# The setup of a fused attention and expert kernel in another order: stages moved on all five engines, other buffers for the raw W1

## Chip, core and metric

The kernel runs on one core of one Trainium2 chip. A core has a matrix engine (TensorE, PE in the profile), a vector engine (DVE), a scalar engine (ACT), GpSimd (POOL) and a synchronisation engine (SP) whose main work here is to issue transfers. Each engine carries out its own instructions in order and waits for others at semaphores. The metric is the time of one execution in microseconds, as the median of several executions.

## What is computed

For each of 32 sequences ("rows") of 512 tokens with 256 channels the reference does a modulated layer norm, a scan over time followed by a 256x256 matrix, a local convolution with 5 taps, a gated residual, a second modulated layer norm, a router that takes one expert of eight by the row's last token, and the expert's two matrices with a GELU between them:

```python
mod = (_silu(L0_c) @ L0_wmod).reshape(L0_c.shape[0], 6, 1, -1)
h = _layernorm(x, axis=-1) * (1 + ca) + sa
x = x + ga * _L0_attn_ref(h, ...)      # scan @ W.T + b + conv(h)
h = _layernorm(x, axis=-1) * (1 + cb) + sb
x = x + gb * _L0_ffn_ref(h, ...)
# in _L0_ffn_ref, per row:
sel = jnp.argmax(action_probs, axis=-1)
h = gelu(einsum('bsh,bhf->bsf', hidden_states, W1[sel]) + b1[sel])
reasoned = einsum('bsf,bfh->bsh', h, W2[sel]) + b2[sel]
return hidden_states + 0.3 * (reasoned @ Wo + bo)
```

## The kernel before

**The loop.** After a setup, `slot(i)` runs for i = 0 to 32 on every engine. In slot i the rows overlap: row i goes through the expert (`up`, `down`), row i+1 through the second norm and the router, row i+2 through the convolution and its residual, row i+3 through the first norm and the scan. The setup must have brought rows 0 to 2 that far. The first matmul of slot 0 after `mix(2)` is `up(0, 0)` (L1011); it needs the expert's first matrix in `up_w`.

**The expert's matrices.** Matrix products are made at higher precision from split operands: a high part (fp32r) and a low part, the difference. The setup makes these tables for all eight experts e:

- W1: SP loads the raw matrix (`load_w1`, L293, 512 KB) into a buffer `w1_nat(e)`, chosen by the table `W1_AT`; ACT writes the high part (`w1_hi`, L538), POOL the low part (`w1_lo`, L414), both into `split_room[e]` (borrowed from `hid_hi`, `hid_lo`, `g_lo`, `down_w` 0 and 1, `up_w` 0 and 1, and `g_lo` again for e = 7); then SP writes the pair (1 MB) to `up_table` in DRAM (`split_out`, L297). A raw buffer is loaded again only when `w1_lo` has read it.
- W2 times Wo: SP or ACT loads W2 (`load_w2`) into row buffer 3, 4 or 5 of `xr`; PE transposes it (`w2_transposes`, L925); ACT copies it (`w2T_copy`, L544); PE multiplies it by Wo (`comb`, L976, two halves per expert); ACT and DVE make high and low parts in `down_tab`, which stays in SBUF (`down_high`, L552; `down_low`, L787).

When all eight splits have landed in `up_table` and the router has chosen row 0's expert (`sel_ready`, L820), SP reads the choice and fetches the expert into `up_w` (L366) and `down_w` (L369).

**The rows in the setup.** A row's first half is: statistics (`stats1`, L745, DVE), inverse deviation (`norm1`, POOL), normalised x (`xn1_of`, L530, ACT), transposes (`to_channels`, L1051, PE), `h_of` (L638, ACT), scan (L826, DVE), split of S (`s_high` on ACT, `s_low0` on POOL L429, `s_low1` on DVE), `mix` (L991 to L995, PE), convolution (`conv`, L797, DVE, ten steps), `gate1` (L589, ACT), `back_to_tokens` (L1043, PE), residual with its statistics (`residual1`, L809, DVE). The second norm is `norm2` (POOL), `xn2_of` (L530, ACT), `to_channels` (PE), `hid_of` (L615, ACT, writes `hid`), `hid_high` and `hid_low`; then `router_nav`, `nav_of`, `router_logits`, `router`.

**What sets the order.** Each engine has a function `prologue()` in which the stages stand in an order written by hand; SP's stands open in its block. Nothing is rearranged by a compiler. Before the change `hid_of(0)` waits until seven `w1_lo` are done, because expert 6's raw W1 lies in `hid`; `split_out(7)` waits for the eighth.

## Time and profile before

| | us |
|---|---|
| three runs, median | 691.85 (689.66 to 692.11) |
| the profiled execution | 695.64 |
| its span, first to last instruction | 693.6 |
| of it, until the first `up(0, 0)` matmul starts | 93.9 |
| mean granted TensorE clock, share of full | 0.984 |

The profiled execution took 2.0 us more than its span, and 3.8 us more than the median. Times in the rows count from the span's start. "Busy" is the time in which an engine had an instruction in work; a wait is idle time before an instruction, with the event that ended it. DMA share is the mean busy share of the 16 DMA engines.

### The profile page before, as it was taken

The numbers are of one execution on the slowest core, as the hardware profiler recorded it, in microseconds if no ns is written. First come the engines' busy times: TensorE is split into PE (matmuls) and PEld (weight loads), VectorE is DVE, ScalarE is ACT, GpSimd is POOL, SyncE is SP. The second block draws the span as 40 slices with busy tenths as digits, with TensorE's granted clock in tenths as the row PEclk, the third lists the DMA queues.
The fourth block names the chain that finished last, engine by engine and source line by source line (L and its number), as shares of the span: only waits on it lengthen the run. The fifth ranks groups of instructions, "written<-read, shape, count | busy, mean of one in ns | idle before, by whom it ended". The sixth has DMA issues, their size and how long they took to land.

```text
span 693.6 us, 11162 instructions
## 1 busy us (share of the span) xinstructions
PE 663.7 (96%) x3469; PEld 532.2 (77%) x3469; DVE 566.3 (82%) x863; ACT 568.4 (82%) x976; POOL 462.8 (67%) x536
## 2 busy tenths in 40 slices
PE   7996759999999999999999999999999999999996
PEld 7985547777777878778777777787877778777764
DVE  1776729999999999999999999999999999998711
ACT  3677548888888998888888888898898888887753
POOL 2743527777777777777777777777777777776543
PEclk9998979999999999999999999999999999999998
DMA  8989345555555554455555555545455555444451
GB/s 265 311 242 314 125 151 157 179 166 168 183 182 160 144 164 167 162 179 179 159 179 161 175 183 181 155 147 177 147 170 183 171 163 183 154 151 152 152 166 47
DMA packets 55454, 120.58 MB, mean 174 GB/s; under 512 B 5643, under 2 KB 43364, under 8 KB 46180
## 3 DMA queue, kind: packets, MB, share of 16 engines
q1 hardware_dynamic: 51844, 115.65, 52.7%
q10 hardware_dynamic: 3552, 4.23, 2.4%
q8 instruction: 28, 0.46, 0.3%
q14 instruction: 30, 0.25, 0.1%
HBM read 61.12 MB, written 25.19 MB: 124 GB/s over the span
## 4 chain that ended last, share of the span: by engine, by line
PE 90%; ACT 2%; DMA 2%; DVE 2%; POOL 2%; issue 1%; POOLq 0%; SPq 0%; DVEq 0%; ACTq 0%
PE Q L1031 9%; PE Q L1026 9%; PE U L1011 9%; PE U L1013 9%; PE U L1012 8%; PE TR L1051 8%; PE Q L1027 8%; PE Y L995 5%; PE Q L1043 4%; PE Y L991 4%; PE Y L992 4%; PE TR L1043 4%; PE Q L976 2%; PE U L1062 2%; PE Y L948 1%
## 5 line engine op out<-in xcount | busy, mean ns | idle before, releaser
L421 POOL TENSOR_TENSOR g_lo<-g,g_hi 128x512 fp32r<-128x512 f32 x128 | 190.8, 1499 | 148.1 <-ACT g_hi L578 142.5
L797 DVE SCALAR_TENSOR_TENSOR Y<-h,taps,Y 128x512 f32<-128x512 f32 x320 | 222.6, 750 | 2.4
L1011 PE MATMUL U<-hid_hi,up_w 128*128 128x512 f32 x256 | 107.1, 418 | 10.2 <-DMA up_w<-up_table 10.2
L571 ACT ACTIVATE g<-U,up_w 128x512 f32<-128x512 f32 x128 | 88.5, 691 | 28.9 <-PE U L1013 26.1
L1026 PE MATMUL Q<-g_hi,down_w 128*128 128x512 f32 x256 | 109.7, 429 | 0.2
L530 ACT ACTIVATE S<-xr,nmr,rstd 128x256 f32<-128x256 f32 x128 | 66.6, 592 | 42.7 <-POOL S_lo L429 36.3
L1013 PE MATMUL U<-hid_lo,up_w 128*128 128x512 f32 x256 | 101.6, 397 | 0.0
L1012 PE MATMUL U<-hid_hi,up_w 128*128 128x512 f32 x256 | 101.3, 396 | 0.0
L1027 PE MATMUL Q<-g_hi,down_w 128*128 128x512 f32 x256 | 101.1, 395 | 0.0
L826 DVE TENSOR_TENSOR_SCAN S<-keep,h 128x512 f32<-128x512 f32 x64 | 75.2, 1215 | 26.7 <-ACT h L638 26.6
L745 DVE BATCH_NORM_STATS2 st<-xr 128x6 f32<-128x512 f32 x128 | 87.6, 706 | 4.3
L1031 PE MATMUL Q<-g_lo,down_w 128*128 128x512 f32 x256 | 83.7, 408 | 0.7 <-POOL g_lo L421 0.7
L578 ACT CAST g_hi<-g 128x512 fp32r<-128x512 f32 x128 | 80.5, 629 | 3.1
L530 ACT ACTIVATE xn<-xr,nmr,rstd 128x256 f32<-128x256 f32 x128 | 66.5, 591 | 8.2 <-POOL nmr L409 6.0
L407 POOL TENSOR_TENSOR rstd<-rstd,minus_half 128x4 f32<-128x4 f32 x64 | 66.4, 1037 | 0.0
L1011 PEld LDWEIGHTS U<-hid_hi,up_w 128*128 128x128 f32 x256 | 48.8, 191 | 19.2 <-DMA up_w<-up_table 10.7
L1031 PEld LDWEIGHTS Q<-g_lo,down_w 128*128 128x128 f32 x256 | 45.0, 187 | 23.7 <-POOL g_lo L421 14.3
L884 DVE SCALAR_TENSOR_TENSOR rT<-Q,mods,w_raw 128x512 f32<-128x512 f32 x64 | 44.6, 739 | 18.1 <-PE Q L1031 18.1
L429 POOL TENSOR_TENSOR S_lo<-S,S_hi 128x512 fp32r<-128x512 f32 x32 | 54.4, 1699 | 5.0 <-ACT S_hi L565 5.0
L1013 PEld LDWEIGHTS U<-hid_lo,up_w 128*128 128x128 f32 x256 | 48.5, 190 | 11.4
L1012 PEld LDWEIGHTS U<-hid_hi,up_w 128*128 128x128 f32 x256 | 49.0, 191 | 8.8
L1026 PEld LDWEIGHTS Q<-g_hi,down_w 128*128 128x128 f32 x256 | 48.1, 188 | 9.8 <-ACT g_hi L578 0.9
(114 smaller groups left out, 1302.7 us busy)
## 6 DMA issues: line engine op xcount, KB each, us to landing
up_w<-up_table SPq DMA_DIRECT2D x32, 1027.0 KB, 6.6
down_w<-down_tab SPq DMA_DIRECT2D x32, 1024.0 KB, 8.6
xr<-in_L_attn_x_dram SPq DMA_DIRECT2D x32, 512.0 KB, 3.6
out_dram<-xr SPq DMA_DIRECT2D x64, 256.0 KB, 2.2
xr<-in_L_ffn_W_dram ACTq DMA_DIRECT2D x5, 512.0 KB, 9.3
xr<-in_L_ffn_W_dram SPq DMA_DIRECT2D x4, 512.0 KB, 6.9
up_table<-g_lo SPq DMA_DIRECT2D x2, 1024.0 KB, 7.9
up_table<-down_w SPq DMA_DIRECT2D x2, 1024.0 KB, 9.6
```

What stands on the lines that cost most here:

```text
L421: nc.gpsimd.tensor_tensor(g_lo[:, f], g[:, f % 2], g_hi[:, f].bitcast(f32), ALU.subtract).then_inc(g_lo_ready, 1)
L530: nc.scalar.activation(to[:, j], xr[:, r % NX, j], ACT.Identity, bias=nmr[:, j:j + 1], scale=rstd[:, j:j + 1]).then_inc(ready, 1)
L571: nc.scalar.activation(g[:, f % 2], U[f % 2][:, :], ACT.Gelu, bias=up_w[:, i % 2, U_B1 + f:U_B1 + f + 1].bitcast(f32)).then_inc(gelu_out, 1)
L578: nc.scalar.copy(g_hi[:, f], g[:, f % 2]).then_inc(g_hi_ready, 1)
L745: return nc.vector.bn_stats(st[:, k * TPB:(k + 1) * TPB].rearrange("p t s -> p (t s)"), pair)
L797: ins = nc.vector.scalar_tensor_tensor(out=Y[c][:, :], in0=h[:, c, k:k + T], scalar=taps[:, c, k:k + 1], in1=Y[c][:, :], op0=ALU.mult, op1 ...
L1011: mm(U[f % 2][:, :], up_w[:, par, UP + w:UP + w + P], hid_hi[:, par, c], start=(c == 0), stop=False)
L1012: mm(U[f % 2][:, :], up_w[:, par, w:w + P], hid_hi[:, par, c], start=False, stop=False)
L1013: ins = mm(U[f % 2][:, :], up_w[:, par, w:w + P], hid_lo[:, par, c], start=False, stop=(c == DC - 1))
L1026: mm(Q[c][:, :], down_w[:, par, 1, w:w + P], g_hi[:, f], start=(f == 0), stop=False)
L1027: mm(Q[c][:, :], down_w[:, par, 0, w:w + P], g_hi[:, f], start=False, stop=False)
L1031: ins = mm(Q[c][:, :], down_w[:, par, 0, w:w + P], g_lo[:, f], start=False, stop=(f == FC - 1))
```

## The change

**Buffers.** `W1_AT` goes from (0, 1, 2, 3, 1, 2, 1, 2) to (0, 1, 2, 0, 3, 1, 2, 4). Place 0 is `rT`, 1 `hid`, 2 `w1_raw[1]`; place 3 was row 2's x buffer and is now `xn`, and the new place 4 is row 3's x buffer. So `rT` is used twice, `hid` holds experts 1 and 5, expert 6 lies in `w1_raw[1]` and expert 7 in row 3's buffer. Row 2's buffer is free for x once the modulations have been computed, row 3's only when the eighth `w1_lo` is done.

**Order.** Stages in the five `prologue()` functions stand in another order; `gbeta`, `hid_gated`, the output and the second residual become functions of their own, called where they were. The work is the same: each load, split, transpose and product once. In short: W2 of expert 0 and the small vectors are loaded first; the vector transpose comes ahead of the modulations; row 0's first transposes come after two experts' W2 transposes; x of row 2 is loaded before `split_out(0)` and its statistics stand ahead of row 0's residual; `w1_lo(7)` on POOL stands ahead of `hid_low(0)` and `w1_hi(7)` on ACT ahead of `xn2_of(0)`; `stats1(3)` stands ahead of `router(0)` on DVE.

```diff
-        W1_AT = (0, 1, 2, 3, 1, 2, 1, 2)
+        W1_AT = (0, 1, 2, 0, 3, 1, 2, 4)
...
 SyncE
-            sp.wait_ge(s_w1_lo, 4)
-            load_x(2)
...
-            load_w1(6)
-            split_out(3)
...
+                sp.wait_ge(s_mod_mm, 1)
+                load_x(2)
+                split_out(0)
+                split_out(1)
+                split_out(2)
+                load_w1(6)
+                split_out(3)
+
+                sp.wait_ge(s_w2T_mm, 4)
+                load_w1(7)
+                split_out(4)
+                load_router()
+                split_out(5)
+                beta_out()
+                split_out(6)
+
+                sp.wait_ge(s_w1_lo, E)
+                load_x(3)
+                split_out(7)
...
 ScalarE, waits of gate1, xn2_of, hid_of (row 0) and of the gated hid
-                    act.wait_ge(s_w1_lo, 1)
+                    act.wait_ge(s_w1_lo, 4)
-                    act.wait_ge(s_wT, 1)
+                    act.wait_ge(s_w1_lo, 5)
-                    act.wait_ge(s_w1_lo, 7)
+                    act.wait_ge(s_w1_lo, 6)
-                        act.wait_ge(s_w1_lo, E)
+                    act.wait_ge(s_w1_lo, 7)
...
 VectorE
-                residual1(0, 1)
-                down_low(3, 1)
-                conv(1, 0, 3)
...
-                conv(1, 3, 6)
-                stats1(2)
...
                 conv(0, 9, 10)
+                stats1(2)
+                down_low(2, 1)
                 scan(1, 0)
...
+                stats1(3)
+                router(0)
...
 TensorE, end of the prologue
                 pe.wait_ge(hid_ready, DC)
                 to_channels(2, xn1, xn1_ready, t1_done)
+                comb(5, 1)
+                w2_transposes(7)
+                back_to_tokens(1)
+                router_nav(0)
                 comb(6, 0)
-                w2_transposes(7)
                 comb(6, 1)
-                router_nav(0)
+                router_logits(0)
                 comb(7, 0)
-                router_logits(0)
-                back_to_tokens(1)
                 comb(7, 1)
```

SyncE's queue, second half of the setup, before. `xr<-in_L_attn_x_dram` is an x load (row 2, then row 3), `hid`, `w_raw` and `xr` from `in_L_ffn_W_dram` raw matrices, `up_table<-` a split going out.

```order
L285 DMA xr<-in_L_attn_x_dram 128x4x256 [waits s_w1_lo]
L338 DMA wp<-in_L_ffn_Wp_dram 128x2x128
L339 DMA wp<-in_L_ffn_Wp_dram 128x8
L340 DMA bp_sb<-in_L_ffn_bp_dram 1x8
L293 DMA hid<-in_L_ffn_W_dram 128x2x512 [waits s_w1_lo]
L297 DMA up_table<-down_w 128x2048 [waits s_w1_lo]
L344 DMA up_table<-beta 128x8x2 [waits s_beta3]
L293 DMA w_raw<-in_L_ffn_W_dram 128x2x512 [waits s_w1_lo]
L297 DMA up_table<-down_w 128x2048 [waits s_w1_lo]
L285 DMA xr<-in_L_attn_x_dram 128x4x256 [waits s_w2T_mm]
L297 DMA up_table<-up_w 128x2048 [waits s_w1_lo] x2
L297 DMA up_table<-g_lo 128x2048 [waits s_w1_lo]
```

The same queue after the change, from the last raw W1 loads to the last split. Row 2's x is no longer in this stretch, it has moved ahead of the first split; the raw W1 of expert 7 goes to a buffer of its own; x of row 3 stands behind seven splits.

```order
L287 DMA xr<-in_L_attn_x_dram 128x4x256 [waits s_mod_mm]
L299 DMA up_table<-hid_hi 128x2048 [waits s_w1_lo]
L299 DMA up_table<-hid_lo 128x2048 [waits s_w1_lo]
L299 DMA up_table<-g_lo 128x2048 [waits s_w1_lo]
L295 DMA w_raw<-in_L_ffn_W_dram 128x2x512 [waits s_w1_lo]
L299 DMA up_table<-down_w 128x2048 [waits s_w1_lo]
L295 DMA xr<-in_L_ffn_W_dram 128x2x512 [waits s_w2T_mm]
L299 DMA up_table<-down_w 128x2048 [waits s_w1_lo]
L328 DMA wp<-in_L_ffn_Wp_dram 128x2x128
L329 DMA wp<-in_L_ffn_Wp_dram 128x8
L330 DMA bp_sb<-in_L_ffn_bp_dram 1x8
L299 DMA up_table<-up_w 128x2048 [waits s_w1_lo]
```

ScalarE around `hid_of(0)`, before. `S<-xr` is `xn1_of(2)`, the casts are `w1_hi(6)` and `w1_hi(7)`, `hid<-TR` is `hid_of(0)`, `g<-U` `w2T_copy(6)`, `h<-TR` `h_of(2)`, `rT<-Y` `gate1(1)`.

```order
L530 ACTIVATE S<-xr,nmr,rstd 128x256 [waits norm1_ready,S_lo_ready1,S_lo_ready0]
L530 ACTIVATE S<-xr,nmr,rstd 128x256 x3
L538 CAST up_w<-hid 128x1024 [waits s_w1_1]
L552 ACTIVATE down_tab<-Q 128x512 [waits s_comb]
L615 ACTIVATE hid<-TR,mods 128x512 [waits t3_done,s_w1_lo]
L615 ACTIVATE hid<-TR,mods 128x512 [waits t3_done]
L544 COPY g<-U 128x512 [waits s_comb,s_w2T_mm]
L544 COPY g<-U 128x512
L552 ACTIVATE down_tab<-Q 128x512 [waits s_comb]
L638 ACTIVATE h<-TR,mods 128x512 [waits conv_done,t1_done] x2
L589 ACTIVATE rT<-Y,mods 128x512 [waits conv_done] x2
L538 CAST g_lo<-w_raw 128x1024 [waits s_split_out1,s_w1_2]
```

The same stretch after the change.

```order
L566 ACTIVATE S<-xr,nmr,rstd 128x256 [waits norm1_ready,S_lo_ready1,S_lo_ready0]
L566 ACTIVATE S<-xr,nmr,rstd 128x256 x3
L574 CAST g_lo<-xr 128x1024 [waits s_split_out1,s_w1_4]
L566 ACTIVATE xn<-xr,nmr,rstd 128x256 [waits norm2_ready,s_w1_lo]
L566 ACTIVATE xn<-xr,nmr,rstd 128x256 x3
L588 ACTIVATE down_tab<-Q 128x512 [waits s_comb]
L651 ACTIVATE hid<-TR,mods 128x512 [waits t3_done,s_w1_lo]
L651 ACTIVATE hid<-TR,mods 128x512 [waits t3_done]
L580 COPY g<-U 128x512 [waits s_comb,s_w2T_mm]
L580 COPY g<-U 128x512
L588 ACTIVATE down_tab<-Q 128x512 [waits s_comb]
L661 CAST hid_hi<-hid 128x512 [waits hid_ready,s_split_out0]
```

Row 2's `xn1_of` and the last `w1_hi` have moved ahead of row 0's `xn2_of`, which stood earlier; `w1_hi(6)` is further up.

GpSimd before, from `w1_lo(5)` to `s_low0(2)`; the four small instructions between are one `norm`.

```order
L414 TENSOR_TENSOR up_w<-w_raw,up_w 128x1024
L404 TENSOR_SCALAR rstd<-st 128x4
L405 TENSOR_SCALAR nmr<-st 128x4
L407 TENSOR_TENSOR rstd<-rstd,minus_half 128x4
L409 TENSOR_TENSOR nmr<-nmr,rstd 128x4
L414 TENSOR_TENSOR up_w<-hid,up_w 128x1024
L461 TENSOR_TENSOR hid_lo<-hid,hid_hi 128x512 x2
L414 TENSOR_TENSOR g_lo<-w_raw,g_lo 128x1024
L429 TENSOR_TENSOR S_lo<-S,S_hi 128x512
```

GpSimd after.

```order
L447 TENSOR_TENSOR up_w<-hid,up_w 128x1024
L437 TENSOR_SCALAR rstd<-st 128x4
L438 TENSOR_SCALAR nmr<-st 128x4
L440 TENSOR_TENSOR rstd<-rstd,minus_half 128x4
L442 TENSOR_TENSOR nmr<-nmr,rstd 128x4
L447 TENSOR_TENSOR up_w<-w_raw,up_w 128x1024
L447 TENSOR_TENSOR g_lo<-xr,g_lo 128x1024
L501 TENSOR_TENSOR hid_lo<-hid,hid_hi 128x512 x2
L462 TENSOR_TENSOR S_lo<-S,S_hi 128x512
```

The eighth `w1_lo` (into `g_lo`) has changed places with `hid_low(0)`, and the norm between the sixth and the seventh is now row 0's second one.

## Rows read from the trace of the kernel before

**Rows 1.** Busy time by window, whole core: setup, then the loop.

```profile
core 0: us, PE busy (x) PEld busy (x) DVE busy (x) ACT busy (x) POOL busy (x), PEclk, DMA share, GB/s
0.00:93.90 93.90, 72.39 (x362) 63.92 (x362) 56.02 (x91) 53.24 (x93) 42.52 (x53) 0.93 0.83 249
93.90:690.00 596.10, 591.10 (x3108) 468.32 (x3108) 509.50 (x771) 515.18 (x883) 420.26 (x483) 1.00 0.51 162
```

**Rows 2.** Waits of TensorE in the setup: total us, times, longest.

```profile
PE U L1011 <- DMA up_w<-up_table: 10.2, 1, 10.2
PE TR L1051 <- ACT hid L615: 5.1, 1, 5.1
...
PE Y L995 <- POOL S_lo L429: 1.5, 1, 1.5
```

**Rows 3.** The chain that ended last, its end in the setup: start, us, what.

```profile
77.46 2.79 POOL g_lo L414
...
80.26 5.62 DMA up_table<-g_lo
...
87.09 6.76 DMA up_w<-up_table
```

**Rows 4.** Timeline of SP's issues: start, us, issue of row 2's x.

```profile
40.57 0.38 SPq L285 DMA_DIRECT2D xr<-in_L_attn_x_dram  x1
```

**Rows 5.** Timeline of DVE: stats2 of row 0, stats1 of row 2, router(0).

```profile
49.90 0.71 DVE L745 BATCH_NORM_STATS2 st<-xr 128x6 f32<-128x512 f32 x1
...
55.79 1.30 DVE L745 BATCH_NORM_STATS2 st<-xr 128x6 f32<-128x512 f32 x2
...
76.69 0.15 DVE L820 FIND_INDEX8 sel<-top,U 1x8 uint32<-1x8 f32 x1
```

**Rows 6.** Timeline of ACT around hid_of(0).

```profile
59.12 2.07 ACT L530 ACTIVATE S<-xr,nmr,rstd 128x256 f32<-128x256 f32 x4 [2.68 <-POOL nmr L409]
61.10 1.03 ACT L538 CAST up_w<-hid 128x1024 fp32r<-128x1024 f32 x1
...
64.24 1.45 ACT L615 ACTIVATE hid<-TR,mods 128x512 f32<-128x512 f32 x2 [1.62 <-POOL up_w L414]
...
67.01 1.52 ACT L638 ACTIVATE h<-TR,mods 128x512 f32<-128x512 f32 x2
68.43 1.44 ACT L589 ACTIVATE rT<-Y,mods 128x512 f32<-128x512 f32 x2
```

**Rows 7.** Timeline of POOL: w1_lo(6), the seventh.

```profile
62.21 2.00 POOL L414 TENSOR_TENSOR up_w<-hid,up_w 128x1024 fp32r<-128x1024 f32 x1 [3.20 <-ACT up_w L538]
```

**Rows 8.** Timeline of PE: second transposes of row 0, one comb pair, mix(2)'s last piece.

```profile
54.84 1.04 PE L1051 MATMUL TR<-ident,xn 128*128 128x128 f32 x8
...
71.78 1.89 PE L976 MATMUL Q<-wo,g 128*128 128x256 f32 x8
...
83.04 0.61 PE L995 MATMUL Y<-S_lo,mix_w 128*128 128x512 f32 x2
```

**Rows 9.** By window, columns as rows 1: DMA share, and TensorE's clock.

```profile
2.00:46.00 44.00, 41.73 (x209) 38.55 (x210) 22.05 (x41) 26.69 (x46) 20.07 (x23) 1.00 0.99 302
46.00:52.00 6.00, 6.00 (x29) 5.16 (x28) 5.90 (x9) 2.87 (x5) 4.83 (x5) 1.00 0.52 144
52.00:73.00 21.00, 15.70 (x80) 13.39 (x79) 12.83 (x18) 15.68 (x27) 6.43 (x8) 0.84 0.96 287
...
64.00:70.00 6.00, 4.26 (x14) 3.79 (x15) 2.77 (x3) 5.76 (x10) 0.21 (x1) 0.50 1.02 380
...
93.90:98.10 4.20, 4.20 (x10) 3.33 (x11) 0.00 (x0) 1.21 (x2) 0.00 (x0) 0.50 0.64 248
```

**Rows 10.** DMA issues to landing, us (last column): W2(5) at 34.85, W2(6) at 45.38, split 7 at 80.26.

```profile
xr<-in_L_ffn_W_dram ACTq DMA_DIRECT2D x1, 512.0 KB, 10.3
```
```profile
xr<-in_L_ffn_W_dram ACTq DMA_DIRECT2D x1, 512.0 KB, 3.5
```
```profile
up_table<-g_lo SPq DMA_DIRECT2D x1, 1024.0 KB, 5.6
```

More of the change, by code:

```diff
@@ L176, in adaln_attention_ffn_kernel @@
         s_wmod = [sem(f"s_wmod{n}") for n in range(NMOD)]
+        s_taps = sem("s_taps")
         s_small = sem("s_small")
-        s_w1 = [sem(f"s_w1_{n}") for n in range(4)]
+        s_w1 = [sem(f"s_w1_{n}") for n in range(5)]
         s_w2 = {n: sem(f"s_w2_{n}") for n in (3, 4, 5)}
@@ new lines, in beta_out, with prologue @@
+            def beta_out():
+                sp.wait_ge(s_beta3, DC)
+                sp.dma_start(up_table.rearrange("e p n -> p e n")[:, :, U_BETA:UPW], beta3[:, :, :]).then_inc(s_params, 16)
+            def prologue():
+                vectors()
+                load_x(0)
+                load_w2(0)
+                load_taps()
+                for_modulations()
+                load_w1(0)
+                load_wo()
+                load_w2(1)
+                load_w()
+                load_x(1)
+                load_w1(1)
+                sp.wait_ge(s_mod_mm, 1)
+                load_w2(2)
+                load_w1(2)
+                b1_out()
+                load_w1(3)
+                sp.wait_ge(s_wT, 1)
+                load_w1(4)
+                load_w1(5)
+                sp.wait_ge(s_mod_mm, 1)
+                load_x(2)
[14 more added lines that the diff above has]
+                split_out(7)
@@ L629, in nav_of, with gate2 @@
                 nc.scalar.activation(nav[:, :], U[1][:, 0:1], ACT.Gelu, bias=vecs[:, V_BP1:V_BP1 + 1]).then_inc(nav_ready, 1)
+            def gate2(r):
+                act.wait_ge(gbeta_ready, r + 1)
+                wait(act, oT_ready, DC * r)
+                if r == 0:
+                    act.wait_ge(s_w1_lo, 7)
+                for c in range(DC):
+                    nc.scalar.activation(hid_gated[:, c], hid_at[r % 2][:, c], ACT.Identity, bias=gbeta[:, c:c + 1],
+                                         scale=col(GB + c, r)).then_inc(hid_gated_ready, 1)
             def h_of(r):
@@ L723, in slot @@
                 if row(i):
-                    act.wait_ge(gbeta_ready, i + 1)
-                    wait(act, oT_ready, DC * i)
-                    if i == 0:
-                        act.wait_ge(s_w1_lo, E)
-                    for c in range(DC):
-                        nc.scalar.activation(hid_gated[:, c], hid_at[i % 2][:, c], ACT.Identity, bias=gbeta[:, c:c + 1],
-                                             scale=col(GB + c, i)).then_inc(hid_gated_ready, 1)
+                    gate2(i)
             prologue()
@@ L814, in residual1, with output, residual2 @@
                 pair_stats(st2, r, k).then_inc(stats2_ready, 1)
+            def output(r):
+                dve.wait_ge(t2_done, HB * min(r + 3, B))
+                for c in range(DC):
+                    dve.wait_ge(hid_gated_ready, DC * r + c + 1)
+                    dve.wait_ge(down_done, DC * r + c + 1)
+                    nc.vector.scalar_tensor_tensor(out=rT[:, c], in0=Q[c][:, :], scalar=col(GB + c, r), in1=hid_gated[:, c],
+                                                   op0=ALU.mult, op1=ALU.add).then_inc(oT_ready, 1)
+            def residual2(r):
+                for k in range(HB):
+                    ts = slice(k * TPB, (k + 1) * TPB)
+                    dve.wait_ge(t4_done, HB * r + k + 1)
+                    nc.vector.tensor_tensor(xr[:, r % NX, ts], xr[:, r % NX, ts], Q[k][:, :].rearrange("p (t d) -> p t d", d=D),
+                                            ALU.add).then_inc(o_ready, 1)
             def router(r):
@@ L832, in prologue @@
                 mods_setup()
+                stats1(1)
                 scan(0, 0)
+                betas()
+                down_low(0, 0)
+                down_low(0, 1)
                 scan(0, 1)
@@ L888, in slot @@
                 if row(i - 1):
[L889 to L894 removed]
+                    residual2(i - 1)
                 if row(i + 2):
```

219 lines of the change are left out of this document (95 added, 124 removed).

## Prediction

> **What bounds the kernel now.** I read the windows first. In the loop PE is busy 591.1 of 596.1 us; in the setup 72.4 of 93.9 [rows 1]. The change leaves the loop's code alone, so a gain can only come from the 93.9 us, and a microsecond by which the first `up(0, 0)` starts earlier is one by which the kernel ends earlier, since PE then runs without a gap. So the question is one moment: when does `up(0, 0)` start.
>
> Next PE's waits in the setup: 10.2 us for the first fetch of `up_w`, 5.1 us for `hid_of(0)`, 1.5 us for the low part of S before `mix(2)` [rows 2]. The rest is below 1 us each, or lies before PE's first input. The chain says what the 10.2 us hang on: POOL's eighth `w1_lo` runs from 77.46 to 80.25, split 7 lands at 85.88, the fetch is issued at 87.09 and lands at 93.85 [rows 3]. The router had chosen at 76.84 [rows 5], and PE had finished `mix(2)` at 83.65 [rows 8]. The last split sets the moment; the router would allow a start 9 us earlier, and PE's own work one at 83.7.
>
> For the 5.1 us: `hid_of(0)` starts at 64.24, released by the seventh `w1_lo` (62.21 to 64.21) [rows 6, 7], although its transposes were done at 55.9 [rows 8]. That `w1_lo` waited for `w1_hi(6)` at 61.10, which stands on ACT behind `xn1_of(2)` at 59.12, which waited for a norm of statistics made only at 55.79 to 57.09 [rows 5, 6], of an x whose load was issued at 40.57 [rows 4]. So a chain of row 2 runs through ACT's order into row 0.
>
> **Part 1: when hid(0) is ready (65.7 before).** By the orders shown, `hid_of(0)` now waits for six `w1_lo`, not seven, and `w1_hi(6)` is not between. Row 2's x is loaded right after the modulations and its statistics (1.3 us) stand after `conv(0)`, some 10 us earlier than before. What remains is row 0's own chain. Its second statistics ended at 50.6 [rows 5]; before them the change both adds and removes: row 0's transposes come after two experts' W2 transposes and W's (20 transposes, of which eight at the warm clock take 0.87 us, so 2.2 us warm, 4.3 us at half clock), `stats1(2)` adds 1.3 us of DVE; in return one comb, the betas and the loads stand elsewhere, and `back_to_tokens(0)` stands after about the same PE work as before. I carried the stages with the durations of the rows and got row 0's second statistics within 1 us of 50.6; I take 51, bounds 49.5 and 54. From there: `norm2` 1.9 us (its end lets `xn2_of` go at 52.9 before); on ACT `xn1_of(2)` 2.07 and `w1_hi(7)` 1.03 [rows 6] now stand between, and they can start only when ACT has finished the copies before, about 51.4. So 51.4 + 2.1 + 1.0 + `xn2_of` 2.1 = 56.6, the last transposes 0.9 behind it, 57.5, `hid_of` 1.45 [rows 6], together **59.5**, bounds 57.5 and 63. The gain up to here is 6.2 us. The 5.1 us of PE's wait go, and the clock with them: PE worked at 0.50 of its clock from 65.7 to 70.9 after that wait (0.50 in the window 64 to 70) [rows 9], which cost half of 5.2, 2.6 us.
>
> **Part 2: from hid(0) to the router's choice (76.84 - 65.7 = 11.1 before).** On ACT the same stages lie between them, less `w1_hi(7)` (1.03). On DVE `stats1(3)` now stands ahead of `router(0)` and adds up to 1.3 us (the same pair of instructions) [rows 5]. `back_to_tokens(1)` and with it `h_of(2)`, `gate1(1)` (1.5 and 1.4) [rows 6] stand ahead of `router_nav(0)`, where before only `hid` and the last copy did; they were on ACT before too, so this costs nothing on ACT and up to 1.7 us of PE's waiting. Sum 11.1 - 1.0 + 1.3 = **11.4**; bounds 10 and 14. The choice comes at 59.5 + 11.4 = 70.9.
>
> **Part 3: the transfers.** The fetch waits for all eight splits. `w1_lo(7)` no longer stands behind `hid_low(0)`, and `w1_hi(7)` needs a raw W1 that no longer waits for an earlier one to be read. On POOL: `norm2(0)` ends at 52.9, two `w1_lo` of 2.0 to 2.8 [rows 3, 7] end at 58 to 59. Before, that was 80.25. So split 7 could be issued 21 us earlier, and then the DMA engines themselves are next. I sum their load: 44 us at 0.99, 6 at 0.52, 21 at 0.96 [rows 9] make 43.6 + 3.1 + 20.2 = 66.9 us of all engines for everything but split 7 and what follows it. One split in a quiet queue lands after 5.6 us [rows 10], of which the chip's best rate in these rows (380 GB/s, rows 9) needs 2.8 us for the bytes. With no gap from 2.0 on, split 7 has moved by 2.0 + 66.9 + 2.8 = 71.7. A landing in a busy queue trails its bytes by a little; estimate 1 us: **72.7**. Bounds: 70 (the 4 us of gaps between other stages stay unused, but overlapping queues count double in the share) and 77 (the gap of 46 to 52, 2.9 us, and another as large open again while SP waits for a `w1_lo` that stands ahead in its queue). So transfers, 72.7, and router, 70.9, come within 2 us of each other; the later one counts.
>
> **Part 4: fetch and start.** From the last landing to the issue 87.09 - 85.88 = 1.2 us, from there 6.8 us [rows 3]. x of row 4 is in the queue ahead of it, as before. 72.7 + 1.2 + 6.8 = **80.7** for `up(0, 0)`. Does PE get there in time? From the end of `hid_of(0)` to the end of `mix(2)` it took 83.65 - 65.7 = 17.9; without 2.6 for the clock and 1.5 for the wait 13.8; one comb (1.73, the start of the next instruction less its own start) [rows 8] has moved behind `hid_of(0)`, 15.5; the 1.7 of part 2 on top, 17.2. 59.5 + 17.2 = 76.7. So PE waits some 4 us for the fetch, against 10.2 before. `down_w` comes 2 to 3 us after `up_w`, and PE has `up(0, 0)`, `up(0, 1)` and transposes to do, as before.
>
> **Part 5: the clock after it.** After the 10.2 us PE ran 4.2 us at 0.50 [rows 9], which cost 2.1 us. A wait of 5.1 us also ended at 0.50, so one of 4 us may end either way: 0 to 2.1 us gained. I take 0.5, nearer to the 5.1 us row.
>
> **The sum.** 93.9 - 80.7 = 13.2, and 0.5: 13.7 us. The profiled execution of 695.64 would become 681.9. The median of the runs stands 3.8 us lower; 691.85 - 13.7 = **678.2**. Stages in the early part that I cost at nothing: the vector transpose ahead of the modulations (vectors issued in the first 3 us), W2 of expert 0 ahead of x(1) (no one needs x(1) before its statistics at some 18), the gates on POOL later (needed by `gate1(0)` only). What covers them is that the DMA engines are full there anyway; without that cover each would cost 1 to 2 us.
>
> **Rivals.**
>
> *The W2 loads starve (start at 84 to 89, gain 5 to 10, 682 to 687).* W2(5) on ACT's queue took 10.3 us while splits were going out on SP's, W2(6) in a quieter stretch 3.5 us [rows 10]. In the new order W2(6) is issued at about 48, into splits 3, 4 and 5, and PE's transposes of it stand ahead of row 0's second transposes. At 3.5 us it lands at 52, at 10.3 us at 58, and PE would need it at 55: 3 us on part 1, and more if other stages slip along. With DMA gaps as in the upper bound of part 3 the start is 77 + 8 = 85. For it: the share is at 0.99 already, and all of this is packed closer. Against it: splits are issued earlier as well, so the load is spread. The Trainium skill, "DMA: Bandwidth & Descriptors", section "Queues, rings and completion order", says that each DMA engine takes turns between queues packet by packet, so a queue with small packets gets less beside one with large ones. By that rule W2 (rows of 1 KB) would get a small part while splits (rows of 8 KB) move, and the 10.3 us would be the case here, with a start near 84; the rows bear it out once, but for one load only.
>
> *The fetch comes as soon as the router allows and PE stays warm (gain over 17, below 675).* If the share counts overlapping packets twice, splits land by 70 and the fetch is issued at 72.1, lands at 78.9, and PE waits 2 us without losing its clock: 93.9 - 78.9 + 2.1 = 17.1, 674.8. PE's own end at 76.7 is the floor: 19.3 us with the clock, 672.6.
>
> *The order gives back what it wins (within 0.5%).* The last stage before `hid_of(0)` could still be late by 9 to 10 us: norm 2 of row 0 behind `w1_lo(5)` on POOL, that behind `w1_hi(5)`, and that behind its raw load. It needs a raw load landing at 50 instead of some 32. Little speaks for it.
>
> *Slower than before (694 to 700): `w1_hi(7)` on ACT.* It now stands ahead of `xn2_of(0)` and waits for splits 2 and 3 to land and for its raw W1; behind it stand all of row 0's second half, the router, and through `hid_ready` PE. Before, it stood behind `gate1(1)`, at 69.8, and nothing of row 0's norm hung on it. Its price is its start less 53.4. It decides against the change from about 68 on: the end of `hid_of(0)` would be at 74, the fetch at 94. Split 3 is issued before W1(7) and needs `w1_lo(3)`, which I have near 35; it would have to land 20 us later than I sum.
>
> **Chances.** Forecast (gain 11 to 17): 0.62. W2 and gaps (5 to 11): 0.22. More than 17: 0.08. Within 0.5%, which is 3.5 us and about what a measurement of this kernel can tell from no change: 0.04. Slower: 0.04. Faster by over 0.5% is the sum of the first three, 0.92. The range leaves out the two last, half of the starving case and half of the best: 673.5 to 685.5.
>
> **What would show it.** In the profile after: the wait for `hid_of(0)` below 1 us and its end near 59.5 (part 1); FIND_INDEX8 near 71 (part 2); the eighth `w1_lo` ending near 59 and split 7 landing near 73, with a DMA share near 1 from 2 to 72 (part 3); `up(0, 0)` near 81 after a wait of 2 to 5 us (part 4); the clock of the 4 us after it (part 5). Wrong would be the forecast if the row period of the loop changed, if DMA share fell below 0.9 in the setup while SP waits, or if PE showed a new wait for a W2 load.

## The result and the profile after

The changed kernel takes 675.15 us, median of 4 runs (675.03 to 676.2); beside it the kernel before took 691.98 (4 runs, 689.66 to 695.5). The ratio is 0.976, with a 95% interval of 0.974 to 0.979: a gain of 16.8 us where 13.7 was forecast. The profiled execution took 675.09 us with a span of 673.0; the one of before had a span of 693.6.

The windows first: the setup up to `up(0, 0)`, the loop, the stretch in which the forecast placed the transfers, the gap behind it, and the first 4 us of the loop. Columns are those of [rows 1].

```profile
core 0: us, PE busy (x) PEld busy (x) DVE busy (x) ACT busy (x) POOL busy (x), PEclk, DMA share, GB/s
0.00:75.14 75.14, 67.72 (x362) 58.78 (x362) 49.59 (x81) 50.63 (x89) 44.11 (x53) 0.91 0.92 310
75.14:673.00 597.86, 589.07 (x3109) 466.39 (x3107) 517.17 (x783) 517.55 (x888) 420.40 (x483) 1.00 0.52 163
2.00:65.00 63.00, 58.51 (x320) 51.78 (x321) 41.98 (x67) 46.38 (x80) 39.45 (x38) 0.89 1.02 345
65.00:70.00 5.00, 4.94 (x26) 3.74 (x25) 4.18 (x10) 1.65 (x4) 1.67 (x4) 1.00 0.03 9
75.14:79.20 4.06, 4.06 (x23) 3.33 (x22) 4.06 (x7) 4.03 (x8) 0.41 (x1) 1.00 0.96 283
```

`up(0, 0)` starts at 75.14, not 93.9 [rows 1]: 18.8 us. The loop behind it takes 597.9 us, not 599.7 (693.6 less 93.9), and its first 4 us run at a granted clock of 1.00, where before they ran at 0.50 [rows 9]: 1.8 us. Together 20.6, the difference of the spans. The medians are only 16.8 apart: the profiled execution of before was 3.8 us above the median of before. Where its time went is told with the run `b_again`.

TensorE's waits in the setup (total us, times, longest), all that are 0.9 us or more:

```profile
PE U L973 <- POOL ident L430: 2.5, 1, 2.5
PE TR L1085 <- ACT rT L625: 1.2, 1, 1.2
PE Q L1018 <- DVE down_tab L826: 1.0, 1, 1.0
PE Y L1037 <- DVE S_lo L843: 0.9, 1, 0.9
PE U L967 <- ACT w_raw L580: 0.9, 1, 0.9
```

The 1.2 us (before 62.09) and the 0.9 us for `S_lo` (before 73.41) lie behind `hid_of(0)`, the others before it. Both long waits of [rows 2] are gone: 10.2 us for the fetch and 5.1 us for `hid_of(0)`. The 2.5 us at the start are those before PE's first input. The timelines of ScalarE, then GpSimd, then VectorE, and of SyncE's issues, where [rows 3 to 7] stood:

```profile
49.85 2.07 ACT L566 ACTIVATE S<-xr,nmr,rstd 128x256 f32<-128x256 f32 x4
51.83 1.03 ACT L574 CAST g_lo<-xr 128x1024 fp32r<-128x1024 f32 x1
52.76 2.08 ACT L566 ACTIVATE xn<-xr,nmr,rstd 128x256 f32<-128x256 f32 x4
55.32 1.45 ACT L651 ACTIVATE hid<-TR,mods 128x512 f32<-128x512 f32 x2
```
```profile
53.01 2.37 POOL L447 TENSOR_TENSOR g_lo<-xr,g_lo 128x1024 fp32r<-128x1024 f32 x1
```
```profile
68.21 0.15 DVE L875 FIND_INDEX8 sel<-top,U 1x8 uint32<-1x8 f32 x1
```
```profile
55.84 0.56 SPq L299 DMA_DIRECT2D up_table<-g_lo  x1
...
69.44 0.36 SPq L398 DMA_DIRECT2D up_w<-up_table  x1
72.88 0.58 SPq L401 DMA_DIRECT2D down_w<-down_tab  x1
```

Three numbers matter. `hid_of(0)` ends at 56.77 (65.7 before). The eighth `w1_lo` ends at 55.38 (80.25 before), and split 7 is issued at 55.84. The router chooses at 68.36 (76.84 before), and the fetch is issued 1.08 us later. The landings, in us from the issue, of split 7 and of that fetch:

```profile
up_table<-g_lo SPq DMA_DIRECT2D x1, 1024.0 KB, 9.1
```
```profile
up_w<-up_table SPq DMA_DIRECT2D x1, 1027.0 KB, 4.8
```

So the splits are all out at 65.0, 3.4 us ahead of the choice; from there to the fetch the DMA engines stand idle (share 0.03 in the window 65 to 70). The fetch lands at 74.24, and PE comes to it at 75.14 straight from `mix(2)`:

```profile
74.67 0.63 PE L1037 MATMUL Y<-S_lo,mix_w 128*128 128x512 f32 x2
75.14 0.39 PE L1053 MATMUL U<-hid_hi,up_w 128*128 128x512 f32 x1
```

The second row has no wait. PE's own work sets the start now, with the fetch 0.9 us ahead of it. What bounded the kernel before, the last split, is off the path by 3.4 us on the way to the fetch.

### The profile page after: what moved, and what is told of

Same layout as the page of the kernel before. It is cut to its first block, busy times and chain, and to the rows that moved or that the text cites. A ratio compares the mean times of both kernels' runs of the same rounds, so it can differ in the third digit from the quotient of the medians.

```text
span 673.0 us, 11162 instructions
## 1 busy us (share of the span) xinstructions
PE 656.8 (98%) x3469; PEld 525.2 (78%) x3469; DVE 566.8 (84%) x863; ACT 568.2 (84%) x976; POOL 464.5 (69%) x536
## 4 chain that ended last, share of the span: by engine, by line
PE 89%; ACT 3%; DVE 2%; DMA 2%; issue 1%; POOL 1%; ACTq 0%; POOLq 0%; SPq 0%; DVEq 0%
PE Q L1073 10%; PE Q L1068 9%; PE U L1053 9%; PE U L1055 9%; PE U L1054 9%; PE Q L1069 8%; PE TR L1093 8%; PE Y L1037 5%; PE TR L1085 4%; PE Q L1085 4%; PE Y L1033 4%; PE Y L1034 4%; PE Q L1018 3%; PE U L1108 2%; DMA xn<-in_L_attn_W_dram 1%
## 5 line engine op out<-in xcount | busy, mean ns | idle before, releaser
L784 DVE BATCH_NORM_STATS2 st<-xr 128x6 f32<-128x512 f32 x128 | 87.7, 706 | 11.4 <-DMA xr<-in_L_attn_x_dram 7.0
```

What stands on the lines that cost most here:

```text
L784: return nc.vector.bn_stats(st[:, k * TPB:(k + 1) * TPB].rearrange("p t s -> p (t s)"), pair)
```

## Experiments

Times are medians; each ratio is to the kernel before on the same chip, with its 95% interval. `up(0, 0)` stands for its start in the trace. "After less" a part means the changed kernel with that part undone.

### The last split alone, in the kernel before (b_swap)

```diff
 GpSimd, end of the prologue (kernel before)
                 w1_lo(6)
-                hid_low(0)
                 w1_lo(7)
+                hid_low(0)
                 s_low0(2)
```

> The kernel before with one edit: on GpSimd the eighth w1_lo stands ahead of hid_low(0). Theory (the last split sets the start of up(0, 0)): w1_hi(7) ended at 70.8, so the eighth w1_lo ends near 73.2 instead of 80.25, split 7 lands near 79, the fetch is issued near 80.2 and lands near 87; up(0, 0) starts 6.9 us earlier than 93.9, the time falls by 6 to 7.5 us. Rival (the transfers are full and the split lands no earlier): no change. Rival (the router sets the fetch): no later than 76.8 + 1.2 + 6.8 = 84.9, a gain of 9.

Measured: 683.35 us, beside 690.42; ratio 0.988 (0.983 to 0.993), a gain of 7.1, where 6 to 7.5 was expected. The chain of work that ended last, its part before `up(0, 0)` (start, us, what):

```profile
67.72 0.94 ACT g_lo L538
...
68.73 2.36 POOL g_lo L414
...
71.11 5.48 DMA up_table<-g_lo
...
77.79 5.30 DMA up_w<-up_table
...
83.13 0.50 PE U L1011
```

One exchange on GpSimd gives some 40% of the gain of the whole change. In this execution `hid_of(0)` starts at 62.10, as in `b_again` (62.32) and not as in the first trace (64.24), so it is set beside `b_again`: the split moves from 77.36 to 71.11, PE's wait for the fetch from 10.3 to 4.5 us, `up(0, 0)` from 91.02 to 83.13; the wait for `hid_of(0)` stays at 5.1. So the chain of [rows 3] was the bound, and after the exchange it still is, with 4.5 us of waiting left. The last split is now held by `w1_hi(7)` on ScalarE, which stands behind `gate1(1)`; that the change moves too.

### After less the early last split (a_late7)

```diff
 GpSimd
                 w1_lo(6)
-                w1_lo(7)
                 hid_low(0)
+                w1_lo(7)
 ScalarE
                 xn1_of(2)
-                w1_hi(7)
                 xn2_of(0)
...
                 gate1(1)
+                w1_hi(7)
                 w2T_copy(7)
 VectorE
-                stats1(3)
                 router(0)
                 down_low(6, 1)
+                stats1(3)
```

> The kernel after with expert 7's split put back: w1_hi(7) behind gate1(1) on ScalarE, the eighth w1_lo behind hid_low(0) on GpSimd, stats1(3) behind router(0). Theory (in the kernel after PE's own work is the bound, with 0.9 us to spare behind the fetch, and the split's early place is what keeps the fetch off the path): the eighth w1_lo ends near 65 instead of 55.4, split 7 lands near 71, the fetch lands near 77, up(0, 0) starts at 77 to 78 instead of 75.1: 2 to 3 us slower than the kernel after. Rival of the prediction (the transfer engines cannot deliver before 72.7 anyway): not slower at all.

Measured: 682.98 us, ratio 0.989 (0.985 to 0.994): 7.8 us slower than the changed kernel, where 2 to 3 was expected. Its chain, the same view:

```profile
66.52 7.32 DMA up_table<-g_lo
...
75.04 6.72 DMA up_w<-up_table
...
81.81 0.80 PE U L1053
```

and the window of the 4 us that follow:

```profile
81.81:85.81 4.00, 4.00 (x9) 3.17 (x10) 1.49 (x3) 1.00 (x2) 0.00 (x0) 0.50 0.71 272
```

Split 7 and the fetch stand behind each other on the path again, and PE waits 5.3 us. The mechanism is the expected one and four sizes were off: split 7 went out at 66.52, not near 65; it took 7.3 us, not 6, with the x loads of two rows around it; the fetch took 6.7, not the 4.8 of the changed kernel; and behind the wait of 5.3 us PE ran at half clock for 4 us. For the fetch the fourteen traces give an order: with `down_w` issued 0.5 us behind it, 6.7 to 6.8 us (three traces); 1.8 and 2.2 us behind, 5.3 (`a_dma3`, `b_swap`); 3.4 us behind, 4.8 to 5.1 (the other nine). The choice itself came at 69.33, only 1.0 later than in the changed kernel. So the rest of the change without the early split gains 7.4 us (682.98 against 690.42), the early split without the rest gained 7.1, and the two ratios multiplied, 0.989 x 0.988, make 0.977, where the whole change had 0.976. The two parts add up. The rest pays even with a late split because the eighth `w1_lo` then stands behind `hid_low(0)`, which moves with `hid_of(0)`.

### After less the early norm of row 2 (a_row2late)

```diff
 VectorE
                 conv(0, 9, 10)
-                stats1(2)
                 down_low(2, 1)
...
                 conv(1, 0, 6)
+                stats1(2)
                 down_low(4, 1)
 GpSimd
                 w1_lo(4)
-                norm1(2)
                 s_low0(1)
                 w1_lo(5)
                 norm2(0)
+                norm1(2)
                 w1_lo(6)
```

> The kernel after with row 2's statistics put back behind the first six steps of conv(1), and its norm on GpSimd behind row 0's second norm. Theory (row 2's chain reaches row 0 through ScalarE's order, since xn1_of(2) stands ahead of xn2_of(0)): statistics at 55 to 56, norm to 58, xn1_of(2) to 60, w1_hi(7) to 61, xn2_of(0) to 63, hid(0) at 65.5 instead of 56.8; PE gets a wait of some 8 us and half its clock behind it; 8 to 11 us slower than the kernel after, 683 to 686. Rival (ScalarE's order matters little, only the last stages wait): up to 3 us slower.

Measured: 685.47 us (9 runs), ratio 0.992 (0.990 to 0.994): 10.3 slower than the changed kernel. ScalarE's timeline (the bracket is its idle time and the releaser):

```profile
57.65 2.07 ACT L566 ACTIVATE S<-xr,nmr,rstd 128x256 f32<-128x256 f32 x4 [8.20 <-POOL nmr L442]
...
60.56 2.07 ACT L566 ACTIVATE xn<-xr,nmr,rstd 128x256 f32<-128x256 f32 x4
...
63.26 1.57 ACT L651 ACTIVATE hid<-TR,mods 128x512 f32<-128x512 f32 x2
```

and TensorE's longest wait:

```profile
PE TR L1093 <- ACT xn L566: 6.2, 1, 6.2
```

ScalarE stands 8.2 us idle before `xn1_of(2)`, a step of row 2, and row 0's `xn2_of` and `hid_of` stand behind it in its order. This is the chain of [rows 4 to 6] made anew: `hid_of(0)` starts 7.9 us later than in the changed kernel, `up(0, 0)` 8.6 later (83.77). The loop behind it is 1.9 us longer, of which PE's wait for the first `down_w` is 0.6. The rest is a fall of the clock 22 us before the end. Eight transposes there, after the same wait for VectorE, in this trace and in the changed kernel:

```profile
661.84 1.66 PE L1085 MATMUL Q<-ident,rT 128*128 128x128 f32 x8 [1.36 <-DVE rT L861]
```
```profile
652.98 1.10 PE L1085 MATMUL Q<-ident,rT 128*128 128x128 f32 x8 [1.37 <-DVE rT L861]
```

From the start of these transposes to the end of the last `up` it takes 11.8 us in the first and 10.3 in the second. The fall stands in five traces (also in `a_dma1`, `a_dma3`, `a_two` and `a_two_w2sp`) and not in the other nine. Why it comes in these is open; it lies 574 us or more behind the start of `up(0, 0)`, and the loops of these five traces are 1 to 1.9 us longer with it than the changed kernel's. The early statistics of row 2 are at least as large a part of the gain as the early split.

### Are the DMA engines full? (a_dma1, a_dma3)

The same 256 KB of weights are written n times to a spare table, behind split 4; n is 4 in `a_dma1` (1 MB) and 12 in `a_dma3` (3 MB). Nothing reads the table.

```diff
 SyncE
                 split_out(4)
+                sp.wait_ge(s_wo, 16)
+                for n in range(12):
+                    sp.dma_start(spare[n], wo...)
                 load_router()
```

> The kernel after with twelve more writes of 256 KB (Wo to a spare table in DRAM, 3 MB) behind split 4 in SyncE's queue. Theory (the engines have 3.4 us to spare before the router's choice, and PE 0.9 us): 8.4 us more of transfer move split 7's landing from 65 to 73, the fetch lands near 79.5, up(0, 0) starts 4 to 5 us later; 3.5 to 6 us slower. Rival (part 3 of the prediction, the engines have nothing to spare): 8 us slower or more.

Measured: 679.91 us, ratio 0.985 (0.981 to 0.990), 4.3 to 4.8 slower than the changed kernel's 675.2 and 675.6. SyncE's queue (start, us, issue):

```profile
40.80 9.15 SPq L380 DMA_DIRECT2D spare<-wo  x12
...
54.11 0.46 SPq L301 DMA_DIRECT2D up_table<-up_w  x1
...
60.53 0.94 SPq L301 DMA_DIRECT2D up_table<-g_lo  x1
...
73.12 0.36 SPq L403 DMA_DIRECT2D up_w<-up_table  x1
```

Split 7 took 11.4 us after its issue and landed at 71.9, the fetch went out 1.2 us later, and PE waited 1.1 us for it. 3.1 MB more moved the last landing by 7.0 us, of which `up(0, 0)` saw 3.3 (78.45 against 75.14): the rest is the slack between the last landing and the choice. But not all of the 7.0 is load on the engines. Twelve issues held SyncE's queue for 9.15 us and the three small loads behind them for 4, so split 5 was issued at 54.11 where it was 49.20. The run shows the slack and not the engines' rate, since it changed both. The time grew by more than the start did, and there the late fall of the clock told above stands in the trace.

> The kernel after with four more writes of 256 KB (1 MB) behind split 4. Theory (the last split lands at 65, 3.4 us ahead of the router's choice, so a third of what cost 4 us with 3 MB hides): split 7 lands near 67.5, the fetch is issued right after the choice as before, 0 to 0.5 us slower than the kernel after. Rival (part 3 of the prediction, the engines are full): 2.8 us slower.

Measured: 676.8 us, ratio 0.978 (0.973 to 0.984), 1.2 to 1.7 above the changed kernel, whose medians (675.15, 675.63) lie within its spread (674.94 to 677.96). The profiled execution was the fastest of the four. In its trace 1 MB more is absorbed: the fetch is issued at 67.94, right behind the choice, and `up(0, 0)` starts at 73.65, 1.5 earlier than in the changed kernel, in part because its modulations ended 0.8 earlier (13.50 against 14.26). Its loop took 599.55 us against 597.9: a wait of 0.4 us for `down_w`, and the late fall of the clock. From 2 to 65 its engines moved 360 GB/s (DMA share 1.04), where the changed kernel's moved 345. So the slack of the last landing is over what 1 MB costs and under what 3 MB and their issues cost.

### The same kernels again (a_again, b_again)

> The kernel after, unchanged, for a second trace beside the others of this call. Theory (the moments at which TensorE's clock rises and falls in the first 25 us differ between executions of the same kernel and move the setup by 1 to 2.5 us): the modulations take 5.3 to 10.3 us in all, whichever clock they meet; up(0, 0) starts between 75 and 77; the median stays within 1.5 us of 675.2. Rival (the early clock of the first trace belongs to the new order): the same 7.9 us for the modulations and 75.1 again.

Measured: 675.63 us, ratio 0.977 (0.975 to 0.979), the result again. The trace differs in its first 25 us. In the changed kernel's first trace, matmuls of the modulation followed each other by 0.11 us up to 9.1 and by 0.21 behind it; in this one by 0.21 throughout. PE reached the first transposes of W2 at 16.84, not 14.26. Yet `hid_of(0)` began at 55.86, not 55.32, the choice came 0.5 later, and `up(0, 0)` at 75.67. Of 2.6 us at the head 0.5 are left, and the rows show where part of the rest goes: comb(0, 0) in the changed kernel's first trace, then in `a_again`.

```profile
21.20 2.64 PE L1018 MATMUL Q<-wo,g 128*128 128x256 f32 x8
```
```profile
22.50 1.89 PE L1018 MATMUL Q<-wo,g 128*128 128x256 f32 x8
```

The execution that was fast early ran longer at half clock behind it. From the next comb (24.49 and 25.04) to the loop the two are 0.5 apart.

> The kernel before, unchanged, for a second trace. Theory (the first trace of before met TensorE's clock late, at 26.7 us, and was 3.8 us above the median for it): up(0, 0) starts at 90 to 93 instead of 93.9, hid(0) is ready 1 to 2.5 us earlier than 65.7, the waits of 5 and 10 us stay. Rival: 93.9 again.

Measured: 692.14 us with a span of 690.0, against 693.6 in the first trace. The waits are those of [rows 2], 10.3 and 5.1; `up(0, 0)` starts at 91.02. Comb(0, 0) in the first trace of before, then in this one:

```profile
23.26 3.57 PE L976 MATMUL Q<-wo,g 128*128 128x256 f32 x8
```
```profile
22.96 1.97 PE L976 MATMUL Q<-wo,g 128*128 128x256 f32 x8
```

They begin 0.3 us apart; one is at half clock to its end, the other is not, and the next comb begins at 27.54 and at 25.64. The same 1.9 us stand at `hid_of(0)` (64.24 and 62.32), 2.9 at split 7 and at `up(0, 0)`. The 1.0 us between them is the clock behind the wait of 5.1 us, which came back earlier in this execution. The comb behind the transposes, in the first trace and in this one:

```profile
67.50 3.57 PE L976 MATMUL Q<-wo,g 128*128 128x256 f32 x8
```
```profile
65.58 2.58 PE L976 MATMUL Q<-wo,g 128*128 128x256 f32 x8
```

The last 0.7 of the 3.6 us between the spans lies in the loop (599.7 and 599.0). The profiled execution on which the prediction rests was the slower of the two. Against `b_again` the span of the changed kernel is 17.0 shorter, which is about the gain of the medians.

### The head of the setup (a_start, a_dum1)

```diff
 SyncE
-                vectors()
                 load_x(0)
+                vectors()
 TensorE
-                vec_transpose()
                 modulation(0)
+                vec_transpose()
```

> The kernel after with the head of the setup put back: x of row 0 ahead of the vectors in SyncE's queue, the vector transpose behind the first modulation. Theory (the head is worth the 0.7 to 1 us by which TensorE begins earlier, most of which the later waits take up again): 0 to 1 us slower than the kernel after. Rival (the head brings the 3.1 us by which the modulations ended earlier in the trace): 2.5 to 3.5 us slower.

Measured: 676.3 us, ratio 0.978 (0.976 to 0.980); 0.7 above `a_again`, and `up(0, 0)` at 76.52, 0.85 later than there. PE waited 3.6 us for its first input, not 2.5. Against the two runs of the changed kernel, 675.15 and 675.63, the head is worth 0.7 to 1.2 us of the 16.8.

The clock then: does denser work bring it up earlier? One transpose without use behind each four matmuls of the modulation:

```diff
                         ins = mm(Y[1][:, m * B:(m + 1) * B], ...)
+                    for q in range(1):
+                        nc.tensor.transpose(TR[0][:, 0:P], ident[:, :], ident[:, :])
```

> The kernel after with one idle transpose (128x128, result unused) behind each pair of modulation matmuls, 24 in all, or 12 where a pair makes two columns. Theory (the small modulation matmuls don't keep TensorE's clock up, and half clock from 9 to 24 us costs the setup time): with denser work the clock is at 2.4 GHz for more of 6 to 24 us, and the later start stages run at full clock; 1 us faster to 1 us slower than the kernel after, since the transposes themselves take 1.3 to 5 us. Rival (the early clock costs nothing, since DMA and the other engines set the pace there): slower by 1 to 3 us.

Measured: 677.63 us, ratio 0.981 (0.979 to 0.984), 2.0 slower than `a_again`. The modulations ended at 18.06, and the W2 transposes behind them still ran at half clock (first row; in the second, from 53.64 of the changed kernel, the same eight transposes are warm):

```profile
18.06 1.91 PE L967 MATMUL U<-ident,xr 128*128 128x128 f32 x8
```
```profile
53.64 1.04 PE L967 MATMUL U<-ident,xr 128*128 128x128 f32 x8
```

In this trace that theory fell. What decides the clock at the head, which differs from execution to execution of one kernel, stays open.

### What bounds it next (a_two, a_w2sp, a_two_w2sp)

Two of the short waits above can be ordered away:

```diff
 VectorE
-                conv(0, 0, 6)
+                conv(0, 0, 4)
                 down_low(1, 1)
-                conv(0, 6, 9)
+                conv(0, 4, 9)
...
                 residual1(1, 1)
+                s_low1(2)
                 down_low(7, 0)
                 down_low(7, 1)
-                s_low1(2)
```

> The kernel after with two stages of VectorE moved: s_low1(2) ahead of down_low(7, 0), and down_low(1, 1) behind four steps of conv(0) instead of six. Theory (TensorE's own work and its short waits are now the bound; two of these waits, 0.9 us for the low part of S before mix(2) and 1.0 us for down_low(1, 1), hang on VectorE's order): up(0, 0) would start 1 to 2 us earlier, but the fetch lands only 0.9 us before it, so 0.5 to 1.5 us faster. Rival (the fetch is the bound as well): no change.

Measured: 676.82 us, ratio 0.978 (0.975 to 0.982), no faster, where 0.5 to 1.5 us was expected. Both waits are gone, and TensorE shows this one:

```profile
55.56 1.09 PE L967 MATMUL U<-ident,xr 128*128 128x128 f32 x8 [3.12 <-DMA xr<-in_L_ffn_W_dram]
```

It waits for W2(6), issued at 43.56, which took 12.0 us to land. In the changed kernel it is issued at 44.59 and takes 8.3; why it takes 3.7 longer here is open. This is the mechanism of the rival "the W2 loads starve", 1 us away from where the change runs. In the changed kernel W2(4) and W2(5), issued on ScalarE's queue at 23.89 and 29.21 while splits go out on SyncE's, take this long:

```profile
xr<-in_L_ffn_W_dram ACTq DMA_DIRECT2D x1, 512.0 KB, 16.3
```
```profile
xr<-in_L_ffn_W_dram ACTq DMA_DIRECT2D x1, 512.0 KB, 16.7
```

Nobody waits for those two there, but they land at 40.2 and 45.9, and PE comes to their transposes at 40.96 and 46.53; W2(6) lands at 52.9, 0.7 us ahead of its own (53.64). Other traces of this order do show the wait: 0.6 us in `a_row2late` and `a_dma3`, 1.1 in `a_dum1`. `a_w2sp` puts the loads of W2(4) to W2(7) between the splits on SyncE's queue, each behind the transposes that free its buffer:

```diff
 SyncE
+                sp.wait_ge(s_w2T_mm, 2)
+                load_w2(4)
                 split_out(0)
                 split_out(1)
+                sp.wait_ge(s_w2T_mm, 3)
+                load_w2(5)
                 split_out(2)
...
                 split_out(4)
+                sp.wait_ge(s_w2T_mm, 5)
+                load_w2(6)
                 load_router()
+                sp.wait_ge(s_w2T_mm, 6)
+                load_w2(7)
 ScalarE
-                if nxt and e != 3:
+                if nxt and e == 0:
                     load_w2(nxt[0])
```

> The kernel after with the W2 loads of experts 4 to 7 issued by SyncE, in line with the splits (4 behind x of row 2, 5 behind split 1, 6 behind split 4, 7 behind the router's weights), instead of by ScalarE. Theory (W2 in 1 KB pieces on ScalarE's queue gets a small part beside the 8 KB pieces of the splits): these loads land within 5 to 10 us instead of 16.3 and 16.7; the kernel is no faster, since no W2 load was waited for in the trace of after; within 1 us of 675.4. Rival (the loads take as long in any queue, since the engines are full): as long as before, and a wait for W2 on TensorE.

Measured: 675.57 us, ratio 0.978 (0.975 to 0.980): as the changed kernel. The same two loads:

```profile
xr<-in_L_ffn_W_dram SPq DMA_DIRECT2D x1, 512.0 KB, 8.3
```
```profile
xr<-in_L_ffn_W_dram SPq DMA_DIRECT2D x1, 512.0 KB, 11.4
```

8 and 5 us less, though the second stayed above the 5 to 10 us that were expected. The bytes are the same, but more than the queue differs. W2(4) now stands ahead of the first two splits, beside which it was issued before. W2(5) stands behind both in either kernel, but no longer behind a W2(4) that is still on its way. So the rows show that these loads take less in line with the splits, and not how much of that is the queue. The Trainium skill, "DMA: Bandwidth & Descriptors", section "Queues, rings and completion order", says that each engine takes turns between its queues packet by packet. If packets of 1 KB rows are the smaller ones, a queue of them gets a small part beside one of 8 KB rows; the two pairs of rows agree with that and do not prove it.

> Both: the W2 loads on SyncE's queue and the two VectorE stages moved. Theory (the two moved stages are worth 1 to 2 us once W2(6) no longer comes late, which cost 3.1 us in the trace with them alone): the wait for W2 is gone, up(0, 0) starts at 73.5 to 74.5 or as early as the fetch allows, 0.5 to 1.5 us faster than the kernel after, 674 to 675, with less spread than 674.2 to 678.7. Rival (another wait takes the place, or the fetch): no faster than after.

Measured: 675.62 us, ratio 0.977 (0.975 to 0.980). The wait for W2 is gone, and `up(0, 0)` starts at 74.92 after a wait of 0.3 us for the fetch, 1.6 us earlier than in `a_w2sp`; the span is only 0.6 shorter (673.8 against 674.4). That last microsecond is the late fall of the clock near the end of the loop, which stands in this trace and not in that of `a_w2sp`. PE's work, the fetch behind the router's choice and W2's landings lie within a microsecond of each other, and no version here beats the changed kernel.

## Why the prediction came out

**The bound.** Right. Only the start of `up(0, 0)` moved, and the loop kept its length but for the clock at its start. `b_swap` and `a_late7` show the chain of the last split from both sides, `a_row2late` the chain of row 2 into row 0.

**Part 1, hid(0) ready.** Forecast 59.5, measured 56.77, below its lower bound of 57.5. The steps are the ones named: `xn1_of(2)`, `w1_hi(7)`, `xn2_of(0)`, the transposes, `hid_of(0)`. Its own terms add up to 58.95 rather than 59.5. Of the remaining 2.2 us, 1.55 is where the group starts (49.85, forecast 51.4), because the combs and copies ahead of it came earlier than carried by hand; and 0.42 is the tail of the transposes: `hid_of(0)` starts 0.48 behind `xn2_of` and not 0.9, with ScalarE busy in between and no wait in its row.

**Part 2, to the choice.** Forecast 11.4, measured 11.6 (68.36 less 56.77). `stats1(3)` does stand directly ahead of the router's MAX8 and FIND_INDEX8 and costs its 1.3 us.

**Part 3, the transfers: the step that failed.** Forecast 72.7 with bounds 70 and 77, measured 65.0. The splits' own chain on GpSimd was forecast to end at 58 to 59 and ended at 55.38. The failure is behind that. I took the share of busy time of the DMA engines, 66.9 us, as work that must be done again. The window 2 to 65 of before and after:

```profile
2.00:65.00 63.00, 56.17 (x285) 50.77 (x285) 37.05 (x62) 37.82 (x66) 31.34 (x34) 0.99 0.96 283
```

against the 1.02 and 345 GB/s shown at the top. At a share that grew by 6% the engines moved 22% more bytes. The share is the time that packets took, and it goes over 1, so packets that overlap are counted each. A share of 0.96 at 283 GB/s was not full. By bytes, [rows 9] make 302 x 44 + 144 x 6 + 287 x 21 = 20.2 MB up to 73, and 1 MB of split 7 on top; at the 345 GB/s reached that is 61.5 us, from 2.0 on 63.5, near the measured 65.0. That sum uses the rate of the stretch that it explains: it says that the work was the same in bytes, not that 345 GB/s is a limit. It is none, as `a_dma1` moved 360 GB/s over the same 63 us. [Rows 9] had a window with 380 GB/s in it, and at that rate the 21.2 MB end at 58 us: a lower bound that could have been worked out before, 12 us below the 70 that the prediction gave. The 1 us by which a landing was to trail its bytes rests on no row, and no run measures it. The prediction held "overlapping queues count double in the share" as the lower bound, 70, and put it 2.7 us below the middle; the landing came nearly 8 below.

**Part 4, fetch and start.** From the choice to the issue 1.08 us (forecast 1.2 behind whatever comes last, and that is now the choice). The fetch took 4.8, not 6.8: I took the duration of [rows 3], where `down_w` followed 0.5 us behind. In the changed kernel `down_w` waits for the last `down_low` (72.06, 0.69 long) and is issued 3.4 us behind. With the choice 2.5 earlier than forecast and the fetch shorter, it lands at 74.24, not 80.7. PE's floor was forecast at 76.7; it came at 75.14, from `hid_of(0)` on 18.4 us and not 17.2. Of these 1.2 us, 0.4 is that two short waits (1.2 and 0.9) make 2.1 where 1.7 was priced, and 0.5 is a comb still in work when `hid_of(0)` ends (to 57.23); 0.3 is spread over the rest. So the order of the two is turned: the forecast had PE waiting 4 us for the fetch, and it waits not at all.

**Part 5, the clock.** I took 0.5 of 0 to 2.1 us. There is no wait, PE's clock is 1.00 in the 4 us that follow, and the loop is 1.8 us shorter.

**The base.** The sum was 13.7; what the two traces show is 20.6, and 3.6 of it is what the first trace of before had over `b_again`: 1.9 us of half clock at comb(0, 0), 1.0 behind the wait for `hid_of(0)`, 0.7 in the loop. I subtracted a gain worked out on the slower execution from the median of the runs. The misses of parts 1, 3, 4 and 5 made the gain too small by 6.9 us and this one made it too large by 3.8, so the forecast came within 3.1 us of the time. That closeness is luck: an error in the base took away half of what the errors in the parts had made. The mechanism in the trace is that of the rival "as soon as the router allows and PE stays warm", to which 0.08 was given. It deserved far more: its condition, that the share counts double, could be read from [rows 9], where a window has a share of 1.02.

**The rivals.** W2(4) and W2(5) did take over 16 us, more than the 10.3 that the rival counted with, but they landed 0.8 and 0.6 us before PE came to them, and W2(6) 0.7. For W2(6) the rival had an issue at 48 and a need at 55; it was issued at 44.59 and needed at 53.64. For the other two the prediction had no sum, and it was close; `a_two` shows that a shift of 1 us at the right place brings the wait back, 3.1 us long. `w1_hi(7)` on ScalarE, the slower case, starts at 51.83, 16 us from where it would decide. `a_row2late` shows the same kind of stall by another entrance: there ScalarE stands 8.2 us idle before the stage ahead of it.

## What to carry to other kernels

When a setup feeds a long loop, look for the one start that counts and for every chain that ends there; here two chains (the last split, and row 2's norm standing ahead of row 0's in an engine's order) cost 7.8 and 10.3 us when undone alone, and the gains of the early split and of the rest, 7.1 and 7.4, add up to nearly the whole. Count transfers in bytes against the best rate that a window of the trace shows, as a lower bound, and not by the busy share. Before a gain from one trace is subtracted from a median, ask whether the part of that trace which makes it unlike the median is a part that the change removes.
